# State-space passes: C rows by DMA, a fourth decay bank, two weighings on GpSimd

## What is computed

```python
xz = einsum('bld,ed->ble', x, in_w); xs, z = split(xz, 2)      # 256 channels each
xs = silu(causal_conv(xs, conv_w) + conv_b)                    # 4 taps
dt, Bc, Cc = split(einsum('bld,ed->ble', xs, xproj_w), ...)    # 8, 16 and 16 columns
dt = softplus(einsum('blr,dr->bld', dt, dt_w) + dt_b)
dA = exp(dt[..., None] * -exp(Alog)); dBx = dt[..., None] * Bc[:, :, None, :] * xs[..., None]
h = dA_t * h + dBx_t;  y_t = sum over the 16 states of h * C_t # over the 64 rows of a sequence
y = (y + Dp * xs) * silu(z);  return einsum('bld,od->blo', y, out_w)
```

## Time and profile before

| | |
|---|---|
| median of 3 runs | 8414.24 us (8408.33 to 8422.7) |
| the profiled execution | 8399.47 us, span 8397.7 us |
| busy: PE, DVE, ACT, POOL | 7059.1, 5556.3, 4193.6, 2659.8 us |
| granted TensorE clock, mean | 0.903 of full speed |

### The profile page before, as it was taken

The page is one execution under the profiler, slowest core; times in us unless marked ns, Lnnn a source line. Parts: engine busy times, 40 slices in busy tenths (PEclk is TensorE's granted clock), DMA queues, the critical chain, the costliest instruction groups (busy, mean ns, idle before and its releaser), DMA issues. The chain is left out here.

```text
span 8397.7 us, 191158 instructions
## 1 busy us (share of the span) xinstructions
PE 7059.1 (84%) x74704; PEld 4348.6 (52%) x74704; DVE 5556.3 (66%) x9325; ACT 4193.6 (50%) x6252; POOL 2659.8 (32%) x1511
## 2 busy tenths in 40 slices
PE   7899888487767778888788886898988999989998
PEld 5676555244332233333333333576755676667676
DVE  7776444555444479999699987365866777767544
ACT  3464333355445556666556556454644444446433
POOL 3211000133220067777577774012611222211000
PEclk9999766599887789999899998999999999999999
DMA  0000000100000011111111110000000000000000
GB/s 25 5 14 10 1 0 0 15 2 3 2 8 0 0 66 65 63 67 66 51 63 66 65 67 31 11 12 7 0 3 27 2 2 2 2 7 14 16 0 20
DMA packets 95253, 185.80 MB, mean 22 GB/s; under 512 B 20328, under 2 KB 54224, under 8 KB 94320
## 3 DMA queue, kind: packets, MB, share of 16 engines
q1 hardware_dynamic: 94832, 179.66, 6.7%
HBM read 172.20 MB, written 5.31 MB: 21 GB/s over the span
## 5 line engine op out<-in xcount | busy, mean ns | idle before, releaser
L2576 POOL TENSOR_TENSOR m_dBx<-m_dtx,m_Bs 128x1024 f32<-128x1024 f32 x518 | 1214.0, 2356 | 449.3 <-DVE m_hs L2895 404.8
L2895 DVE TENSOR_TENSOR_SCAN m_hs<-m_ps_dA,m_dBx 128x512 f32<-128x512 f32 x1036 | 1207.9, 1207 | 160.1 <-ACT m_ps_dA L2777 90.9
L2687 PE MATMUL m_ps_y<-m_yc,ident 128*128 128x512 f32 x2072 | 1061.1, 638 | 0.0
L2777 ACT ACTIVATE m_ps_dA<-m_dt,m_A 128x504 f32<-128x504 f32 x1036 | 682.8, 678 | 487.0 <-DVE m_hs L2895 477.6
L2903 DVE TENSOR_TENSOR m_yc<-m_hs,m_ps_C 128x1024 f32<-128x1024 f32 x518 | 622.3, 1201 | 68.2 <-PE m_ps_C L2670 67.7
L2687 PEld LDWEIGHTS m_ps_y<-m_yc,ident 128*128 128x128 f32 x2072 | 423.8, 206 | 362.4 <-issue 334.2
L2223 POOL TENSOR_TENSOR a_s<-a_s,a_den 128x1024 f32<-128x1024 f32 x128 | 243.6, 1903 | 1142.6 <-DVE a_den L2269 1142.6
L2670 PE MATMUL m_ps_C<-m_parts,m_sel 128*128 128x512 bf16 x520 | 209.5, 403 | 397.4 <-DVE m_yc L2903 396.0
L2670 PEld LDWEIGHTS m_ps_C<-m_parts,m_sel 128*128 128x128 bf16 x520 | 50.2, 97 | 663.8 <-DVE m_yc L2903 606.0
L2267 DVE TENSOR_REDUCE a_den<-a_s 128x16 f32<-128x1024 f32 x128 | 156.0, 1219 | 207.5 <-ACT a_s L2175 207.5
L2054 PEld LDWEIGHTS a_ps_out<-a_wo,a_oT 128*128 128x128 f32 x2048 | 239.6, 192 | 103.1 <-ACT a_oT L2179 103.1
(11 more groups left out here) (739 smaller groups left out, 17134.8 us busy)
## 6 DMA issues: line engine op xcount, KB each, us to landing
m_Bs<-m_B_rows SPq DMA_DIRECT2D x260, 512.0 KB, 3.6
c_kvb<-in_ctxT SPq DMA_DIRECT2D x68, 128.0 KB, 2.1
c_kvb<-in_ctxT SPq DMA_DIRECT2D x17, 256.0 KB, 2.7
out_dram<-X SPq DMA_DIRECT2D x1, 4096.0 KB
m_B_rows<-m_low SPq DMA_DIRECT2D x34, 32.0 KB, 3.1
c_table<-in_table SPq DMA_DIRECT2D x2, 512.0 KB
x_xr<-X SPq DMA_DIRECT2D x8, 128.0 KB, 4.8
x_pT<-in_ctx SPq DMA_DIRECT2D x8, 128.0 KB
```

What stands on the lines that cost most here:

```text
L2576: return nc.gpsimd.tensor_tensor(to, one, other, ALU.mult)
L2687: last = nc.tensor.matmul(ps_y[:, m, :], C.ident[:], yc[:, s % 2, m, :], start=s == 0, stop=s == NS - 1)
L2777: nc.scalar.activation(seqs(ps_dA[:, h % 3, :]), seqs(dt[:, par, m, :]), ACT.Exp, scale=A[:, m, s:s + 1]).then_inc(decay, 1)
L2895: nc.vector.tensor_tensor_scan(hs[:, s % HS, m, :], ps_dA[:, (2 * s + m) % 3, :], dBx[:, s % BX, m, :], 0.0, ALU.mult, ALU.add).then_inc(s ...
```

## The change

The 16 C rows are stored with the B rows and spread to SBUF by one transfer for each state, `Cs`, four slots; the product with `sel` and the split into `parts` go. Their PSUM bank becomes a fourth bank of decays. The weighings of states 3 and 6 move to GpSimd, into a buffer `yp` of their own, and TensorE adds these two at steps 5 and 8. `dtx` has one slot instead of two. The skip term is added at step 7. Constants and SyncE:

```diff
-    SLOTS, CHUNK, BX, HS = 4, 2, 4, 4
-    FREE_HALVES, FREE_STATES, FREE_ROWS = 3, SLOTS * CHUNK, 1
+    SLOTS, CHUNK, C_SLOTS, BX, HS, BANKS = 4, 2, 4, 4, 4, 4
+    FREE_HALVES, FREE_STATES, FREE_ADDS, FREE_ROWS = BANKS, SLOTS * CHUNK, NS, 1
+    SKIPPED = 7
+    POOL_WEIGHS = (3, 6)
+    DVE_WEIGHS = [s for s in range(NS) if s not in POOL_WEIGHS]
+    ADDED_AT = {3: 5, 6: 8}
+    ADD_ORDER = [s for step in range(NS) for s in ([step] if step not in POOL_WEIGHS else []) +
+                 [w for w in POOL_WEIGHS if ADDED_AT[w] == step]]
...
+        def adds_through(s):
+            return FREE_ADDS + ADD_ORDER.index(s) + 1
+        def C_at(j, s):
+            return j * (16 * NS // C_SLOTS) + (s // C_SLOTS * 16 + 16)
...
+            def spread_C(j, par, s):
+                back = NS if s < C_SLOTS else 0
+                sp.wait_ge(y_added, j * NS - back + adds_through((s - C_SLOTS) % NS))
+                sp.dma_start(Cs[:, s % C_SLOTS, :], bc(BC_rows[par, NS + s:NS + s + 1, :],
+                                                       [P, GT])).then_inc(C_loaded[s % C_SLOTS], 16)
             with sp.Fori(0, C.NG // 2) as pair:
                 for par in range(2):
-                    store_B(pair * 2 + par, par)
+                    store_rows(pair * 2 + par, par)
                     for c in range(NS // CHUNK):
                         spread_B(pair * 2 + par, par, c)
+                        for s in range(CHUNK * c, CHUNK * c + CHUNK):
+                            spread_C(pair * 2 + par, par, s)
```

GpSimd:

```diff
+            def weigh(j, s):
+                rank = POOL_WEIGHS.index(s)
+                pool.wait_ge(scanned, j * (2 * NS) + (2 * s + NHF + FREE_HALVES))
+                pool.wait_ge(C_loaded[s % C_SLOTS], C_at(j, s))
+                if rank:
+                    pool.wait_ge(y_added, j * NS + adds_through(POOL_WEIGHS[rank - 1]))
+                else:
+                    pool.wait_ge(y_added, j * NS + adds_through(POOL_WEIGHS[-1]) - NS)
+                hold()
+                multiply(yp[:], hs[:, s % HS, :, :], bc(Cs[:, s % C_SLOTS, :].unsqueeze(1), both)).then_inc(yp_ready, 1)
...
                     for s in range(AHEAD, NS):
                         state(i, s, par)
+                        if s - BX in POOL_WEIGHS:
+                            weigh(i, s - BX)
                         front(i + 1, s, 1 - par)
```

TensorE:

```diff
-            def spread_C(s, par):
-                nc.tensor.matmul(ps_C[:], sel[:, s, :], parts[:, par, :], start=True, stop=True).then_inc(C_done, 1)
+            def add_states(i, step):
+                if step not in POOL_WEIGHS:
+                    add_state(i, step)
+                for s in POOL_WEIGHS:
+                    if ADDED_AT[s] == step:
+                        add_state(i, s)
```

ScalarE, in `state` and `front`:

```diff
-                    back = 3 if h >= 2 else 2
-                    act.wait_ge(scanned, j * (2 * NS) + (h - back + 1 + FREE_HALVES))
+                    act.wait_ge(scanned, j * (2 * NS) + (h - BANKS + 1 + FREE_HALVES))
...
-                    nc.scalar.activation(parts[:, par, :], ps_j[:], ACT.Copy).then_inc(high_ready, 1)
```

VectorE, where `front` with its four operations goes, and a scan waits for the weighing that frees its slot of `hs`:

```diff
+                    weighed = (s - HS) % NS
+                    back = 1 if s < HS else 0
+                    if weighed in POOL_WEIGHS:
+                        dve.wait_ge(yp_ready, j * NPW + (POOL_WEIGHS.index(weighed) + 1 - back * NPW))
...
             def weigh(j, s, wait_free=True):
+                if s in POOL_WEIGHS:
+                    return
-                dve.wait_ge(C_done, j * NS + (s + 1))
-                nc.vector.tensor_tensor(yc[:, s % 2, :, :], hs[:, s % HS, :, :], bc(ps_C[:].unsqueeze(1), both),
-                                        ALU.mult).then_inc(yc_ready, 1)
+                dve.wait_ge(C_loaded[s % C_SLOTS], C_at(j, s))
+                nc.vector.tensor_tensor(yc[:, rank % 2, :, :], hs[:, s % HS, :, :],
+                                        bc(Cs[:, s % C_SLOTS, :].unsqueeze(1), both), ALU.mult).then_inc(yc_ready, 1)
```

More of the change, by code:

```diff
@@ L2503, in mamba @@
         low = sb("low", [P, GT])
-        parts = sb("parts", [P, 2, GT], BF16)
         x, e, r, v, ln = (sb(n, [P, NHF, GT]) for n in ("x", "e", "r", "v", "ln"))
         q = e
-        dt, dtx = sb("dt", [P, 2, NHF, GT]), sb("dtx", [P, 2, NHF, GT])
-        Bs = sb("Bs", [P, SLOTS, CHUNK, GT])
+        dt, dtx = sb("dt", [P, 2, NHF, GT]), sb("dtx", [P, NHF, GT])
+        Bs, Cs = sb("Bs", [P, SLOTS, CHUNK, GT]), sb("Cs", [P, C_SLOTS, GT])
         dBx = sb("dBx", [P, BX, NHF, GT])
-        hs, yc = sb("hs", [P, HS, NHF, GT]), sb("yc", [P, 2, NHF, GT])
-        ps_dA, ps_C, ps_y = ps("ps_dA", [P, 3, GT]), ps("ps_C", [P, GT]), ps("ps_y", [P, NHF, GT])
+        hs, yc, yp = sb("hs", [P, HS, NHF, GT]), sb("yc", [P, 2, NHF, GT]), sb("yp", [P, NHF, GT])
+        ps_dA, ps_y = ps("ps_dA", [P, BANKS, GT]), ps("ps_y", [P, NHF, GT])
         ps_j, ps_k = ps("ps_j", [P, GT]), ps("ps_k", [P, GT])
@@ L2607, in front @@
                 elif s == 15:
-                    multiply(dtx[:, par, :, :], dt[:, par, :, :], xs[:, par, :, :])
+                    pool.drain()
+                    multiply(dtx[:], dt[:, par, :, :], xs[:, par, :, :])
                     pool.drain()
@@ L2683, in project, with add_state @@
                 last.then_inc(out_done, 1)
-            def add_state(s):
+            def add_state(i, s):
+                if s in POOL_WEIGHS:
+                    pe.wait_ge(yp_ready, i * NPW + (POOL_WEIGHS.index(s) + 1))
+                    of = yp
+                else:
+                    rank = DVE_WEIGHS.index(s)
+                    pe.wait_ge(yc_ready, i * NDW + (rank + 1 + FREE_ROWS))
+                    of = yc[:, rank % 2, :, :]
                 for m in range(NHF):
-                    last = nc.tensor.matmul(ps_y[:, m, :], C.ident[:], yc[:, s % 2, m, :], start=s == 0, stop=s == NS - 1)
+                    last = nc.tensor.matmul(ps_y[:, m, :], C.ident[:], of[:, m, :], start=s == 0, stop=s == NS - 1)
                 last.then_inc(y_added, 1)
+            def add_states(i, step):
[4 more added lines that the diff above has]
+                        add_state(i, s)
             def front(j, s, par, in_loop):
@@ L2875, in _ @@
             dve.drain()
[L2877 to L2887, removed]
             def scan(j, s, in_prologue=False):
                 if s >= HS or not in_prologue:
-                    dve.wait_ge(yc_ready, j * NS + (s - HS + 1 + FREE_ROWS))
+                    weighed = (s - HS) % NS
+                    back = 1 if s < HS else 0
+                    if weighed in POOL_WEIGHS:
+                        dve.wait_ge(yp_ready, j * NPW + (POOL_WEIGHS.index(weighed) + 1 - back * NPW))
+                    else:
+                        dve.wait_ge(yc_ready, j * NDW + (DVE_WEIGHS.index(weighed) + 1 - back * NDW + FREE_ROWS))
                 dve.wait_ge(dBx_ready, j * NS + (s + 1 + FREE_STATES))
@@ L3993, in layouts @@
         low[:, 32:32 + DTR] = m("xproj_w")[:DTR].T
[L3994 to L3996 removed]
+        low[:, 0:2 * NS] = m("xproj_w")[DTR:].T
+        a[d + "_xp"], a[d + "_out_w"] = halves(low[:, :64]), halves(m("out_w").T)
         a[d + "_dt_w"], a[d + "_A"] = np.ascontiguousarray(m("dt_w").T), halves(m("Alog"))
```

89 lines of the change are left out of this document (38 added, 51 removed).

## The result

The changed kernel takes 9125.4 us (median; 9120.55 to 9136.42), the kernel before 8411.28 beside it (8400.51 to 8422.7): a ratio of 1.085, 95% interval 1.0837 to 1.0863. That is 714 us slower. Forecast were 8930 us and a range of 8520 to 9080: the direction and both mechanisms held, the size was 195 us short, and the time lies above the range.

A forecast was written before the change was run, and what follows sets the result against it. VectorE bounds the kernel before at 64.8 us per group; turns with GpSimd and B transfers queued behind C rows make it 81: 16.2 x 32 = 518 us on 8399.5 gives 8918, plus 15 is 8932, put as 8930; range 8520 to 9080.

The forecast's parts named there:

- turns: In the state-space passes, VectorE weighings reading two SBUF operands and GpSimd exclude each other: 14 x 0.98 us of GpSimd per group.
- ties: Waits for turns where either VectorE or GpSimd may start first: 77.7 to 84.9 us per group, middle 81 taken.
- (a): From scan 8: GpSimd's operations, adds of states 8 and 6, then issue and landing of B chunk 6, at 17.2 us.
- (b): GpSimd full from the product of state 12 to the next group's state 0: nine operations, five drains, five turns, 27.2 us.
- (c): VectorE's next scans 0 to 3, three weighings, `q` and `Y`: 14.2 us, plus waits of 1.2 and 1.7.
- (d): VectorE from the next group's weighing of state 2 through that of state 5, which waits 2.3 for GpSimd: 13.0 us.
- (e): Adds of states 5 and 3 (3.6 us), issue (0.5), B landing (4.0), product of state 8 (2.3), to next scan 8.
- slow adds: In (e), TensorE's adding matmuls may run at a low clock after idling: 1.6 us more per group (86.5).
- Turns alone: Rival: transfers arrive early enough, so the period is the shared sum, 68.3 us: about 8525 us; chance 0.10.
- Transfers alone: Rival: VectorE and GpSimd do not exclude each other, only late transfers cost, +7.2 us per group: about 8645; chance 0.07.
- Faster: Rival: queue keeps ahead, turns fall in GpSimd's waits for scans; period 54.6 to 56 us, about 8110; chance 0.08.
- No change: Rival: gain and cost cancel within 0.4 us per group, about 8414 us; chance 0.02.

## Why the forecast was right in kind and short in size
**Both mechanisms are there.** From the changed kernel, freeing the queue gives 9125 - 8626 = 499 us and then removing the turns 8626 - 8221 = 405; the rest is what the change saves, 8411 - 8221 = 190: 499 + 405 - 190 = 714. (The three runs are single ones, and the second and third stood beside a kernel before of 8406.) In the other order the turns give 185 and the queue 8937 - 8221 = 716. So the two hide each other in part: a turn that falls while GpSimd would wait for B costs nothing. The single prices of rivals have to be read with that.

**Turns.** The 0.98 us was near: GpSimd's operations with a turn take 2.7 to 3.4 instead of 2.34, most of them 3.1 or more, and 302 us over 341 of them is 0.89 each. With the queue free, the turns cost 13.2 us per group in the first pass (72.5 - 59.3), 10.4 in the second (71.3 - 60.9), and 405 / 32 = 12.7 over the kernel, where 14 x 0.98 = 13.7 was laid out. The Trainium skill's page SBUF — State Buffer, section Who interferes with whom, is borne out in the pair of engines and in the exception (an operand in PSUM ends it). Read as the prediction read it, as 1.22 us of GpSimd's time per turn, it is too much: 0.89 to 0.98 were measured.

**The layout, leg by leg.** Measured in the group shown, from the `dBx` of state 12 at 3582.86 to that at 3670.16, and in the mean over 30 such stretches of both passes. w is a weighing on VectorE, st a `dBx`, a prime marks the next group:

| leg | laid out | as forecast, ties halved | measured | mean of 30 |
|---|---|---|---|---|
| (a) scan 8 to B 6 landed | 17.2 | 16.2 | 19.6 | 19.0 |
| (b) st12 to scan 0' | 27.2 | 27.2 | 25.8 | 25.8 |
| (c) to the end of scan 3' | 17.1 | 15.7 | 17.9 | 18.8 |
| (d) to the end of w5' | 13.0 | 11.9 | 12.05 | 12.2 |
| (e) to scan 8' | 10.4 | 10.4 | 12.0 | 11.9 |
| sum | 84.9 | 81.3 | 87.3 | 87.6 |

**The step that failed** is "I take the middle, 81, since nothing in the trace decides ties". It took off 3.6 us per group, 115 us of the kernel. The ties did not split. Over the kernel VectorE's weighings took 747.7 us instead of 454 x 1.20, which is 6.4 us of turns per group, against 7.2 with all ties lost and 3.6 as forecast. In the group shown the weighing of state 7 took 3.24 us, that of state 15 3.30 (at 3610.91) and that of state 2' 2.84 (at 3626.53); behind that of state 15 the product `q` then waited 1.60 more for its adds.

They also fell on other weighings than laid out (8, 0', 1' and 5'), and the two largest were no ties at all. The weighings of states 7 and 15 lose 2.0 and 2.1 us in every one of the 32 groups. Each follows a pair of scans that began just after its `dBx` had ended, some 0.2 us after GpSimd had gone on to the next product. GpSimd's boundary after that comes 2.30 us later, the scans take 2.25: the weighing arrives 0.13 to 0.18 us after GpSimd has started again (3652.84 against 3652.66, and 3610.91 against 3610.78), and waits for nearly the whole of it. Spacings of 2.25 and 2.31 stood in the prediction.

In (d) and (e) the path was another than laid out. The weighing of state 5' at 3637.39 ran at full length, and this saved nothing: it delayed GpSimd's weighing of state 3, for whose add the queue waits just as much. I had counted that tie as a gain of 2.3 without asking what the loser does. GpSimd's weighing of state 3 was late already, behind chunk 3 of B, and it is what `C(7)` waited for last, not VectorE's weighing as laid out. So it is in part luck that 13.0 for (d) is near the 12.05 measured: without any turns (d) and (e) together took 26.4 us (13.2 and 13.2, below), more than the 24.1 here with them.

**The other 2.4 us per group**, 77 us, are the rest of the sum: +2.4 in (a), +0.8 in (c), +1.6 in (e), against -1.4 in (b) and -1.0 in (d). Issue to start of the product was 4.76 and 4.72 us instead of 4.0, once in (e) and once in (a): three or four C rows and a second B chunk leave within 3 us of it, and the DMA engines are nearly full while they land, as in this stretch, in which chunk 6 lands ahead of leg (b):
```profile
3579.00:3585.00 6.00, 3.71 (x9) 1.43 (x8) 1.23 (x1) 1.96 (x3) 2.14 (x1) 1.00 0.93 311
```
(DMA share 0.93, 311 GB/s). The median landing of B is 4.4 us, had 3.6; that the crowding is the reason was not tried by itself. In (a) the add of state 6 ended 14.0 us after scan 8 instead of 12.7, the slow adds above (13.2 in the mean), and a second C row ahead of the chunk made the issue 0.84 instead of 0.5. In (e) chunk 4 left 4.7 us after the weighing of state 5', where 4.1 was laid out, behind GpSimd's delayed weighing. Against these stands (b), with four turns instead of five. Single periods lie between 85.5 and 90.1 us. In the first pass the seven groups in which scan 3 waits for its decay have 88.5 to 90.1 us, and (c) is 20.7 to 22.6 there instead of 17.9; the others, but for the first, have 85.8 to 87.7. The prediction had waits for decays near zero.

**The range** reached to 9080 from 84.9 us. The bound of slow adds, 86.5 us, stood in the text as +1.6 and gives 8399.5 + 15 + 21.7 x 32 = 9109; the prediction says that its range takes in the slow adds, but 9080 does not reach that bound, and 9125 lies just above it.

**The rivals.** *Turns alone* (8525) came out at 8626: the same price per turn, but GpSimd still waits 191.5 us, 6.0 per group, for scans, where the shared sum has it wait for nothing. *Transfers alone* (8645) came out at 8937, a period of 81.6 (first pass) instead of 72.0. Its legs (a) to (e) were 16.9, 22.6, 15.8, 13.2 and 13.2 against 15, 22.3, 14.2, 10.1 and 10.4. It missed most in (d), where scans 4 to 7 each wait 0.3 to 1.8 us, that of state 6 for chunk 3, which left late behind two C rows, and in (e), from the weighing of state 5 to scan 8. *Faster* (8110) needs both causes gone, and then is 8221. *No change* was never near.

**Costed at nothing.** The fourth bank (9122 without it) rightly. The two late adds were laid out and not costed at nothing, but as one term among others. They are the larger part of the queue's 499 us: without the two weighings the queue costs 8756 - 8540 = 216, so 283 hang on them.

## What to carry to other kernels
A semaphore wait in an in-order DMA queue is a wait of everything behind it: before an operand is moved to a transfer, write down what each entry of the queue waits for, and free a slot when it has been read, not when the result has been used. An operand in PSUM may be what keeps two engines apart, so moving it to SBUF has a price even where the instruction takes the same time alone. When a layout has ties, first compare the spacings of the two sides from their last common start: two of these ties were lost in every group by 0.2 us. Then follow the loser of each: if it stands on the same path the tie saves nothing.

## What was not expected of the hardware
- A collision costs GpSimd 0.4 to 1.1 us (2.7 to 3.4 instead of 2.34; 0.89 in the mean) and VectorE up to 2.2 (3.39 instead of 1.20); over two thirds of VectorE's 454 weighings still took 1.20.
- Where both start within 0.01 us, VectorE ran at full length and GpSimd paid the turn, as at 3637.39 and 3637.40, and so it was in all 89 such pairs of the two passes (weighings of 1.20 us, GpSimd's operation over 3.0).
- With 256 KB transfers queued around it, a 512 KB one lands in 4.4 us at the median instead of 3.6; where three or four leave together, the product that waits for it starts 4.7 to 4.8 us after the issue.
